# Two message-passing layers on one core: messages, gather counts and sums by the pair of tiles instead of by the tile

## What is computed

```python
x_t = _mlp2(x, W1n, b1n, W2n, b2n)
e_t = _mlp2(edge_attr, W1e, b1e, W2e, b2e)
aggregated = jax.ops.segment_sum(x_t[src] * e_t * dp_scale, dst, num_segments=num_nodes)
out0 = _norm(x + aggregated * res_w) * gamma + beta
x = _layernorm(x + out0)
xw = jnp.einsum('ni,rio->rno', x, jnp.einsum('rb,bio->rio', w_comp, weight))
node = jax.nn.relu(jax.ops.segment_sum(xw[etypes, src] * norm, dst, num_segments=N) + h_bias)
return _layernorm(x + node)
```

## Time and profile before

| | us |
|---|---|
| median of 3 runs | 4970.07 (4955.96 to 4988.68) |
| the profiled execution | 4952.68 |
| its span, first to last instruction | 4950.8 |
| mean granted clock of TensorE | 0.664 |

### The profile page before, as it was taken

How to read it: one execution, slowest core, us unless ns; L and a number is a source line. 1 busy time by engine, 2 the same in 40 slices (tenths; PEclk the granted TensorE clock), 3 DMA queues, 4 the chain that set the end, 5 groups by cost and what they waited for, 6 DMA issues and landing times.

```text
span 4950.8 us, 32349 instructions
## 1 busy us (share of the span) xinstructions
PE 2223.0 (45%) x6997; PEld 1406.5 (28%) x6998; DVE 1644.3 (33%) x3785; ACT 324.7 (7%) x686; POOL 2989.6 (60%) x3218
## 2 busy tenths in 40 slices
PE   5555555556556656565665222332322333323333
PEld 5333333333333333333332111121211222212222
DVE  4233333333333334343442122322322233223333
ACT  2000000001111111110111000000000000000000
POOL 6566665656565555555543676666666666666664
PEclk8677777777777777777775555555555556555565
DMA  4111111111111111111111111111111111111111
GB/s 102 30 32 33 33 32 43 32 42 43 42 43 41 37 42 42 42 52 42 51 38 39 23 25 23 22 24 24 24 25 24 25 24 27 25 25 25 24 28 21
DMA packets 199560, 169.74 MB, mean 34 GB/s; under 512 B 82780, under 2 KB 135152, under 8 KB 199250
## 3 DMA queue, kind: packets, MB, share of 16 engines
q0 software_dynamic: 100032, 102.60, 11.0%
q1 hardware_dynamic: 98930, 64.45, 4.3%
q10 hardware_dynamic: 288, 0.07, 0.0%
HBM read 134.80 MB, written 32.10 MB: 34 GB/s over the span
## 4 chain that ended last, share of the span: by engine, by line
another core or an unknown queue 43%; issue 27%; DVE 11%; PE 10%; DVEq 5%; ACT 1%; ACTq 1%; POOL 1%; DMA 0%; SPq 0%; POOLq 0%
DVE acc L1008 3%; PE ps_agg L1388 3%; DVE work L1088 3%; DVE work L997 2%; PE ps_fin L1477 2%; PE ps_z L1364 1%; DVEq L987 1%; PE ps_o L1380 1%; POOL rows L595 1%; DVEq L1022 1%; DVEq L1008 1%; PE ps_agg L1477 1%; ACT low L656 1%; DVEq L997 1%
## 5 line engine op out<-in xcount | busy, mean ns | idle before, releaser
L595 POOL DMA_INDIRECT rows<-node_table,acc x1523 | 1437.9, 944 | 1009.9 <-DVE work L1088 556.9
L595 POOL DMA_INDIRECT rows<-rel_table,row_ix x1563 | 1476.8, 945 | 861.7 <-issue 480.5
L1388 PE MATMUL ps_agg<-work 128*128 128x256 f32 x2348 | 895.2, 529 | 1520.5 <-DVE work L1088 1080.9
L1388 PEld LDWEIGHTS ps_agg<-work 128*128 128x128 f32 x2348 | 582.5, 264 | 1855.1 <-DVE work L1088 1172.4
L1008 DVE TENSOR_TENSOR acc<-acc,ps_agg 64x128 f32 x1174 | 328.9, 280 | 914.6 <-remote 722.0
L1055 DVE SCALAR_TENSOR_TENSOR hid<-ps_z,b1e_c,low 128x512 f32<-128x512 f32 x196 | 147.2, 751 | 1304.0 <-ACT low L656 1041.1
L997 DVE TENSOR_TENSOR work<-ps_x,rel 128x1024 f32<-128x1024 f32 x392 | 479.0, 1222 | 277.6 <-issue 231.3
L1364 PE MATMUL ps_z<-attrT,W1e_d 128*128 128x256 f32 (+1 forms) x784 | 376.3, 613 | 7.4 <-ACT enorm L747 7.4
L1088 DVE TENSOR_TENSOR work<-rows,ps_o 128x256 f32<-128x256 f32 x782 | 323.1, 413 | 78.1 <-DMA rows<-rel_table,row_ix 46.0
L1388 PE MATMUL ps_z<-work 128*128 128x256 f32 x392 | 172.6, 585 | 371.8 <-DVE work L1088 205.6
L1388 PE MATMUL ps_T<-work 128*128 128x256 f32 x388 | 169.3, 582 | 322.0 <-issue 176.3
(11 more groups left out here) (137 smaller groups left out, 1083.7 us busy)
## 6 DMA issues: line engine op xcount, KB each, us to landing
rows<-rel_table,row_ix POOLq DMA_INDIRECT x1563
attr<-in_edge_attr_dram SPq DMA_DIRECT2D x39, 640.0 KB
rows<-node_table,acc POOLq DMA_INDIRECT x1523
rel_table<-acc SPq DMA_DIRECT2D x19, 1280.0 KB
node_table<-work SPq DMA_DIRECT2D x24, 128.0 KB, 2.0
out_dram<-x_sb SPq DMA_DIRECT2D x19, 160.0 KB
x_sb<-in_x_dram SPq DMA_DIRECT2D x1, 768.0 KB, 7.1
acc<-in_dst_dram SPq DMA_DIRECT2D x1, 768.0 KB
```

The source lines that it names most:

```text
L595: nc.gpsimd.indirect_dma_start(rows[0:n, t % BODY, j, :], None, table, bass.IndirectOffsetOnAxis(ap=lists[0:n, t, j : j + 1], axis=0),).th ...
L1388: last = nc.tensor.matmul(bank[:, 0 : 2 * P], data[:, 2 * jj : 2 * jj + 2, :], hot[:, 2 * jj : 2 * jj + 2, :], start=(jj == 0), stop=(jj = ...
```

## The change

- A pair has one message instruction of 128x512 instead of two of 128x256, one semaphore `gathered` for its eight gathers (5 in place of 10 for each layer), one count `msg_ready`, and one count `scattered` after its fourth matmul.
- The two tiles' sums stand side by side in one bank of 512 columns: `ps_agg0` for every pair of layer 0, `ps_agg0` and `ps_agg1` in turn in layer 1. The second tile's additions still follow the first's.
- DVE's step changes. In layer 0, both additions of pair p come before the one-hot and the message of pair p + 1, and the message of pair p's second tile, which stood behind `edge_hidden(p + 2)`, now belongs to that single message one step earlier; the wait for the edge products moves ahead of the transposition. In layer 1, the whole message of pair p + 1 comes before the wait for pair p's sums.
- `rel_products` uses `ps_agg1` and loses its wait for an addition; the chunk's 14 linked steps get a semaphore each and are compared with one number for each chunk.

```diff
--- before.py
+++ after.py
@@ -228,10 +228,10 @@
...
         iota_ps = ps_x[:, 2 * P : 3 * P]
-        ps_xT = ps_T[:, V * P : (V + 1) * P]
-        sums = [[[ps_agg0, ps_agg1], [ps_agg0, ps_agg1]], [[ps_agg0, ps_agg1], [ps_z, ps_T]]]
+        ps_xT = ps_T[:, 0:P]
+        sums = [[ps_agg0, ps_agg0], [ps_agg0, ps_agg1]]
...
-        ps_rel = [ps_fin, ps_agg0]
+        ps_rel = [ps_fin, ps_agg1]
@@ -287,27 +287,27 @@
...
-        gathered = [[sem(f"gathered{l}_{u}") for u in range(BODY)] for l in range(2)]
+        gathered = [[sem(f"gathered{l}_{u}") for u in range(HALF)] for l in range(2)]
...
-        msg_ready = [[sem(f"msg_ready{l}_{v}") for v in range(V)] for l in range(2)]
+        msg_ready = [sem(f"msg_ready{l}") for l in range(2)]
...
-        scattered = [[sem(f"scattered{l}_{v}") for v in range(V)] for l in range(2)]
+        scattered = [sem(f"scattered{l}") for l in range(2)]
...
         x_added = [sem(f"x_added{l}") for l in range(2)]
-        chunk_steps = sem("chunk_steps")
+        chunk_step = [sem(f"chunk_step{k}") for k in range(14)]
@@ -321,7 +321,7 @@
...
         MSG_LEAD, HID_LEAD, MM1_LEAD = 3, 1, 1
-        MM2_LEAD, SUM_LEAD, ADD_LEAD = 1, 2, [2, 3]
+        MM2_LEAD, SUM_LEAD, ADD_LEAD = 1, 2, [[2, 2], [2, 3]]
@@ -588,14 +588,14 @@
...
-                    pool.wait_ge(msg_ready[l][t % V], (t - BODY) // V + 1 + MSG_LEAD)
+                    pool.wait_ge(msg_ready[l], (t - BODY) // V + 1 + MSG_LEAD)
@@ -1013,15 +1013,18 @@
...
 
-                dve.wait_ge(scattered[l][v], count(p, 0, SUM_LEAD))
-                add_window(window_of(u, v), sums[l][u % 2][v], 0).then_inc(added[l][v], 1)
+                if v == 0:
+                    dve.wait_ge(scattered[l], count(p, 0, SUM_LEAD))
+                else:
+                    dve.wait_ge(added[l][0], count(p, 0, ADD_LEAD[l][0]))
+                add_window(window_of(u, v), sums[l][u % 2], v * 2 * P).then_inc(added[l][v], 1)
...
@@ -1061,32 +1064,35 @@
                 if u % HALF == 0:
                     dve.wait_ge(attr_loaded[u // HALF % 2], (turns + 1) * 16)
                     dve.sem_inc(turns_begun, 1)
+
+                if not is_fixed(p) or p >= 3:
+                    products_of(p - 2)
                 nc.vector.transpose(attrT[:, :], attr[:, u // HALF % 2, u % HALF, :]).then_inc(attr_turned, 1)
 
-            def message(l, p, u, v):
-                slot = u % HALF * V + v
+            def products_of(p):
+                dve.wait_ge(mm2_done, count(p, 0, MM2_LEAD))
+
+            def message(l, p, u):
+                slot, n = u % HALF, width(p) * J
                 if is_fixed(p):
-                    of_tile = TILE_GATHERS if p < LAST else 16 * (TAIL_FULL + 1)
-                    dve.wait_ge(gathered[l][slot], p // HALF * TILE_GATHERS + of_tile)
+                    of_pair = PAIR_GATHERS if p < LAST else 16 * (TAIL_FULL + 1)
+                    dve.wait_ge(gathered[l][slot], p // HALF * PAIR_GATHERS + of_pair)
                 else:
                     if slot == 0:
-                        dve.reg_add(landed, landed, TILE_GATHERS)
+                        dve.reg_add(landed, landed, PAIR_GATHERS)
                     dve.wait_ge(gathered[l][slot], landed)
-                tile = rows[:, slot, :, :]
+                tiles = rows[:, slot * V : slot * V + width(p), :, :].rearrange("p t j f -> p (t j) f")
                 if l == 0:
-                    if v == 0:
-                        dve.wait_ge(mm2_done, count(p, 0, MM2_LEAD))
-                    factor = ps_o[u % 2][:, v * J * F : (v + 1) * J * F].rearrange("p (j f) -> p j f", f=F)
+                    factor = ps_o[u % 2][:, 0 : n * F].rearrange("p (j f) -> p j f", f=F)
                 else:
                     if slot == 0 and is_fixed(p):
                         dve.wait_ge(weights_staged, p // HALF + 1)
                     elif slot == 0:
                         dve.reg_add(staged, staged, 1)
                         dve.wait_ge(weights_staged, staged)
-                    factor = ps_o[u // HALF % 2][:, slot * J : (slot + 1) * J].rearrange(
-                        "p (j o) -> p j o", o=1).to_broadcast([P, J, F])
-                nc.vector.tensor_tensor(
-                    msg[:, u % 2, v * J : (v + 1) * J, :], tile, factor, ALU.mult).then_inc(msg_ready[l][v], 1)
+                    factor = ps_o[u // HALF % 2][:, slot * V * J : slot * V * J + n].rearrange(
+                        "p (j o) -> p j o", o=1).to_broadcast([P, n, F])
+                nc.vector.tensor_tensor(msg[:, u % 2, 0:n, :], tiles, factor, ALU.mult).then_inc(msg_ready[l], 1)
 
...
@@ -1110,12 +1116,12 @@
...
+                rounds = c + (l * CHUNKS + 1) if is_fixed(c) else dve.snap(c + (l * CHUNKS + 1))
 
                 def link_c(ins):
+                    ins.then_inc(chunk_step[taken[0]], 1)
+                    dve.wait_ge(chunk_step[taken[0]], rounds)
                     taken[0] += 1
-                    ins.then_inc(chunk_steps, 1)
-                    first = c * STEPS0 if l == 0 else c * STEPS1 + CHUNKS * STEPS0
-                    dve.wait_ge(chunk_steps, first + taken[0])
...
@@ -1184,16 +1190,15 @@
...
                     edge_hidden(p + 2)
-                if not is_fixed(p) or p > 0:
-                    dve.wait_ge(added[0][1], count(p, -1, ADD_LEAD[1]))
-                message(0, p, u, 1)
                 if not is_fixed(p) or p + 3 <= LAST:
                     attr_turn(p + 3, (u + 3) % TURN, i + (u + 3) // TURN)
-                add_sums(0, p, u, 0)
-                dve.wait_ge(added[0][0], count(p, 0, ADD_LEAD[0]))
+                else:
+                    products_of(q)
+                for v in range(V):
+                    add_sums(0, p, u, v)
+                dve.wait_ge(added[0][1], count(p, 0, ADD_LEAD[0][1]))
                 main_one_hot(q, n % 2)
-                message(0, q, n, 0)
-                add_sums(0, p, u, 1)
+                message(0, q, n)
@@ -1202,14 +1207,11 @@
...
                 if not is_fixed(p) or p > 0:
-                    dve.wait_ge(added[1][1], count(p, -1, ADD_LEAD[1]))
+                    dve.wait_ge(added[1][1], count(p, -1, ADD_LEAD[1][1]))
                 main_one_hot(q, n % 2)
-                message(1, q, n, 0)
-                add_sums(1, p, u, 0)
-                dve.wait_ge(added[1][0], count(p, 0, ADD_LEAD[0]))
-                if width(q) == V:
-                    message(1, q, n, 1)
-                add_sums(1, p, u, 1)
+                message(1, q, n)
+                for v in range(V):
+                    add_sums(1, p, u, v)
@@ -1383,10 +1385,10 @@
...
 
-            def sum_by_target(data, hot, bank):
+            def sum_by_target(data, hot, bank, at):
                 for jj in range(2):
                     last = nc.tensor.matmul(
-                        bank[:, 0 : 2 * P], data[:, 2 * jj : 2 * jj + 2, :], hot[:, 2 * jj : 2 * jj + 2, :],
+                        bank[:, at : at + 2 * P], data[:, 2 * jj : 2 * jj + 2, :], hot[:, 2 * jj : 2 * jj + 2, :],
@@ -1401,11 +1403,11 @@
...
+                pe.wait_ge(msg_ready[l], count(p, MSG_LEAD))
                 for t in range(width(p)):
-                    pe.wait_ge(msg_ready[l][t], count(p, MSG_LEAD))
                     of_tile = slice(t * J, (t + 1) * J)
-                    sum_by_target(msg[:, r, of_tile, :], onehot[:, r, of_tile, :], sums[l][r][t]).then_inc(
-                        scattered[l][t], 1)
+                    last = sum_by_target(msg[:, r, of_tile, :], onehot[:, r, of_tile, :], sums[l][r], t * 2 * P)
+                last.then_inc(scattered[l], 1)
                 with pe.While(lambda: pe.snap(further) > 0):
@@ -1455,10 +1457,9 @@
             def finish1(c):
                 finish(1, c)
 
-            def rel_products(c, pairs, part=None):
+            def rel_products(c, part=None):
                 lo, hi = part or (0, blocks_in(c))
 
-                pe.wait_ge(added[0][0], pairs + ADD_LEAD[0])
                 pe.wait_ge(normed[0], c + 1)
```

More of the change, by code:

```diff
@@ L1498, in _ @@
             for l in range(2):
-                for v in range(V):
-                    pe.sem_inc(msg_ready[l][v], MSG_LEAD)
+                pe.sem_inc(msg_ready[l], MSG_LEAD)
             edge_first(0)
@@ L1511, in half0 @@
                         part_of_chunk(
-                            pe, tabled, limit, k, PART_AFTER.index(u), lambda c, part: rel_products(c, first + (u + 1), part))
+                            pe, tabled, limit, k, PART_AFTER.index(u), rel_products)
             pe.reg_mov(lead, 4)
@@ L1522, in _ @@
             step0(first + 1, 1, LOOPS)
[L1523 removed]
+            next_chunk(pe, tabled, limit, BODIES - 1, rel_products)
             step0(first + 2, 2, LOOPS)
@@ L1526, in _ @@
             step0(first + 3, 3, LOOPS)
-            next_chunk(pe, tabled, limit, BODIES, lambda c: rel_products(c, first + 4))
+            next_chunk(pe, tabled, limit, BODIES, rel_products)
             step0(first + 4, 4, LOOPS)
```

37 lines of the change are left out of this document (18 added, 19 removed).

## The result

| | before | after |
|---|---|---|
| median, us | 4979.38 (4955.96 to 4996.13, 4 runs) | 5170.82 (5156.25 to 5204.09, 4 runs) |
| ratio | | 1.0427 (95%: 1.0394 to 1.0459) |
| span of the profiled execution | 4950.8 | 5154.4 |

The forecast was 4915 us with a range to 5060. The profiled execution after took 5156 us; the third rival ("the longer way to the message") had put it at 5142 us.

The account below looks back on a forecast made before the run. POOL's gathers and its waits for DVE's message, delayed by late PE counts, were taken to bound the kernel. 4952.68 - 18 (layer 0) - 14 (layer 1) - 5 (between layers) = 4915.7 us, range 4780 to 5060.

Parts of the forecast that it names:

- the longer way to the message: Rival, both layers: each stop is paid with 3.4 us of additions, one-hot and message; 5142 us, chance 0.20.
- What bounds the kernel: Whole kernel: POOL's gathers and issue, 3840 us, plus waits for DVE's message, held up by PE counts arriving late.
- One message, fewer instructions: DVE's message in both layers: one of 0.75 us replaces two of 0.41, counted as nothing because DVE waits anyway.
- One count: PE's `scattered` and the gathered signal, one per pair: the saving of the count itself put at 0.
- the rival by which counts are slow: Rival, both layers: each PE count takes its turn, so fewer counts save 350 us; 4603 us, chance 0.05.
- Order in layer 0: Layer 0's message moved behind additions and one-hot: stops of 6.4 to 8.3 us instead of 5.04, but later; -18 us.
- the cycle of 35.5 us: Layer 0 when the third message is on time: 29.9 + 2.2 + 3.4 us for three pairs, 11.8 a pair.
- the two to one: Layer 0's weighting of 11.8 us a pair (third message on time) against 13.1 (late), giving 12.27 against 12.36 before.
- The 25 rows: Layer 0: PE counts are on time for 25 rows of matmul after POOL resumes; those behind were late.
- Layer 1: Some 40 stops: 14 doubles gain 3.2 us each, 26 singles grow by 1.2; -14 us in all.
- The change of layers: Between the layers, with POOL idle and counts on time: 5 pairs some 1 us shorter each, -5 us.
- A late count with POOL idle for more than 3 us would break the whole account: Sign for the profile after: a count still late with POOL idle over 3 us would refute the account of late counts.

Follow-up runs that it names:

- y1: The changed kernel, nothing edited, in a session where no count was late: 4074.98 us beside 4075.22 for the kernel before, ratio 0.9999.
- x2: The kernel before with a spare count on every product of the loops that had none, in a session without late counts: ratio 1.0000.
- x8: The kernel before with a spare count on every product of the loops that had none, in a session with late counts: ratio 0.9994.
- z2: The changed kernel with late counts forced by making DVE wait in two pairs of five until POOL's last gather has landed: 4973.50 us.
- z1: The kernel before with late counts forced by making DVE wait in two pairs of five until POOL's last gather has landed: 4543.19 us.
- z4: The changed kernel with forced late counts, its message directly behind `hid` in layer 0 and ahead of the one-hot in layer 1: 4632.45 us.
- w1: The changed kernel with the message directly behind `hid` in layer 0, ahead of the one-hot in layer 1; late counts unforced: 5012.08 us, 1.0154 to kernel before.
- x5: The kernel before with two small uncounted bf16 products ahead of each tile's sums, in a session with late counts: ratio 1.0208.

## Why the prediction was wrong

- **What bounds the kernel** held, with one thing missing. POOL and its waits for the message are the time, and PE's late counts end them. That the lateness belongs to a session and not to the kernel (4067 us without it) no row of one execution could show; I had taken it as given. The forecast and the 4.3% hold only where counts are late.
- **One message, fewer instructions**: priced at nothing; it takes 0.675 us, 0.75 was forecast, and where no count is late it changes nothing (y1).
- **One count**: priced at 0. x2 and x8 add counts instead of taking them away and show 0, which refutes the rival by which counts are slow.
- **Layer 0, the step that failed.** It is the price of a stop in "Order in layer 0": the release and the way from the late count to the message. The longer way was seen and sized: "5.3 us behind a late count for ACT, 3.4 us where only `scattered` is late"; it is 5.27. But the cycle of 35.5 us was summed with the two cheap ends, a release of 2.2 us and the way of 3.4, though rows 4 gave most of the waits to ACT. With 2.97 + 5.3 it would have been 38.2 us, 12.7 a pair and +70 us; it measured 4.28 + 5.27, 39.2 us and 13.06 a pair. The release came later, not sooner. The stops with products of `rel_products` were in no term, neither at their price before (7.3 to 10.5 us) nor with the way of 7.9 us that the change gives them: twelve of them take 201 us. The third message was on time as often as forecast: the 41 runs of 24 hold 984 of the loop's 1523 gathers, close to the two to one that it was given. Instead of -18 us the layer gave +152.
- **The 25 rows.** "A count 10.3 us late right behind the 25th row" reads rows 6 too closely: nine rows of `edge_second` and four of `edge_first` come after the 25th, and the late count is that of the last four.
- **Layer 1**: forecast -14, measured +56. The layer had some 56 stops before, not 40. They became fewer by 8, not by 14, since two stops a pair apart still follow each other (16 of the 48); and one stop grew by 2.4 us by z2 - z1, not 1.2, because the kernel before is released by the first tile's two additions and message.
- **The change of layers**: -5 forecast, -5.3 measured.
- **The rival that came true** had the right mechanism. That its sum (5142 us) came so near is in part luck: it had runs of 16 with a way of 3.4, and the stops that made the loss come mostly behind runs of 24, with a way of 5.3 or 7.9.
- "A late count with POOL idle for more than 3 us would break the whole account": releases of 4.28 and 5.70 us are there. By this sign the account had failed; what failed of it is the 2.97 us as a constant. The price of the way held in z1 to z4 and w1.

## What to carry to other kernels

Where an engine is let go by another's count, lay the two orders side by side and add up everything between the count that comes last and the signal that the waiting engine needs. Merging per-tile work into per-pair work saves instructions and can lengthen exactly that way. When one branch of a sum has two prices, take the one that the profile's waits mostly show. And where the bound engine only waits because its buffers are out, let it wait for the late event itself a little earlier, so that the work between passes beside it: it cost nothing here without late counts and gave 3.2% with them.

## What the runs showed of the hardware

- The same kernel on the same kind of chip takes 4067 or about 4950 us from one session to the next, all runs of a kernel within a session agreeing to 1%; chips 9 and 10 showed both. In the longer one PE's counts reach ACT, DVE and POOL late while POOL issues indirect gathers (23.0 us in the stop at 1107.25 of the kernel after, 10.3 in rows 6), and those that are still out when POOL stops came 2.8 to 5.7 us after its last gather had ended in the stops shown. POOL's gathers (0.944 and 0.947 us) and issue (0.30) are the same in both.
- It does not grow with PE's counts (x8, 0.9994); with instructions added on PE the time grew by 1.4% beyond their own cost (x5). What makes a session of either kind was not found. One thing that could hold PE back is the path of the engines' records: by the Trainium skill (NOTIFIC — the notification-queue block, section "7.1 Overflow: three behaviours, one of which stalls the engine") the block's internal pipeline holds its producers back rather than lose a record. No run here shows whether that is it.
